# Seeding the scores' bank from VectorE instead of by a matmul, and a second bank for the values

## What is computed

```
# first: 128 latent tokens look at 2048 context tokens + the 128 latents, 16 heads of 64, batch 4
kv  = concat([xn @ Wkv, ln @ Wkv]);  k, v = split(kv)
qn, kn = rmsnorm(q) * scale, rmsnorm(k)
attn = softmax(qn @ kn.T  (masked));  out = attn @ v
# second: 128 tokens look at 2048 context tokens, 16 heads of 32, batch 4
score = (q @ k.T) / sqrt(32), masked with -1e9;  out = softmax(score) @ v
```

## Time and profile before

| | us |
|---|---|
| median of 3 runs | 2676.53 (2675.3 to 2676.94) |
| the profiled execution, its own time | 2673.37 |
| its span, first to last instruction | 2671.6 |
| mean granted TensorE clock | 0.948 of full speed |
| busy: PE, DVE, ACT, POOL | 2347.0, 1645.9, 1592.9, 1115.5 |

### The profile page before, as it was taken

How to read it: one execution, slowest core, us unless ns; L and a number is a source line. 1 busy time by engine, 2 the same in 40 slices (tenths; PEclk the granted TensorE clock), 3 DMA queues, 4 the chain that set the end, 5 groups by cost and what they waited for, 6 DMA issues and landing times. The chain is left out here.

```text
span 2671.6 us, 57444 instructions
## 1 busy us (share of the span) xinstructions
PE 2347.0 (88%) x21892; PEld 1526.2 (57%) x22210; DVE 1645.9 (62%) x3086; ACT 1592.9 (60%) x2934; POOL 1115.5 (42%) x896
## 2 busy tenths in 40 slices
PE   5389999999999999998688699995799899996885
PEld 2245666666666665655345477773567676774442
DVE  4466666666666655554146399995777777763126
ACT  3246666666666666666225288984477777777103
POOL 2345666556755675446100000003466666656000
PEclk9599999999999999999889799997999999997887
DMA  4322233223322231111352479994533434221302
GB/s 129 96 73 78 67 112 91 71 71 115 91 71 69 83 89 39 38 39 34 115 206 70 155 283 364 363 337 169 165 116 117 125 116 130 86 87 53 106 0 81
DMA packets 256291, 314.10 MB, mean 118 GB/s; under 512 B 71425, under 2 KB 182913, under 8 KB 255121
## 3 DMA queue, kind: packets, MB, share of 16 engines
q1 hardware_dynamic: 252064, 302.28, 35.4%
q10 hardware_dynamic: 3312, 6.03, 0.6%
q0 software_dynamic: 640, 2.10, 0.3%
HBM read 226.56 MB, written 48.10 MB: 103 GB/s over the span
## 5 line engine op out<-in xcount | busy, mean ns | idle before, releaser
L602 POOL TENSOR_TENSOR a_plo<-a_p,a_phi 128x512 bf16<-128x512 f32 x272 | 331.1, 1218 | 406.0 <-ACT a_phi L658 403.8
L788 PE MATMUL ps<-w_lo,a_xhi 128*128 128x512 bf16 x1078 | 409.7, 380 | 2.0 <-issue 0.2
L787 PE MATMUL ps<-w_hi,a_xhi 128*128 128x512 bf16 x1054 | 400.5, 380 | 2.6
L789 PE MATMUL ps<-w_hi,a_xlo 128*128 128x512 bf16 x1039 | 394.7, 380 | 0.5
L1937 POOL TENSOR_TENSOR a_plo<-a_p,a_phi 128x512 bf16<-128x512 f32 x256 | 303.1, 1184 | 179.9 <-ACT a_phi L1974 175.1
L624 ACT ACTIVATE a_kraw<-ps 128x256 f32<-128x256 f32 x272 | 104.2, 383 | 381.3 <-PE ps L789 378.7
L681 DVE TENSOR_TENSOR a_v<-ps,a_v 128x256 bf16<-128x256 f32 x272 | 114.7, 422 | 327.7 <-ACT a_v L626 327.5
L2069 DVE CUSTOM_DVE_ANT_0 a_junk<-ps,a_biasrow 128x512 bf16<-128x512 f32 x256 | 176.2, 688 | 115.6 <-PE ps L2184 88.1
L1969 ACT ACTIVATE a_p<-ps,a_mcol 128x512 f32<-128x512 f32 x256 | 174.9, 683 | 93.7 <-PE ps L2202 87.1
L561 POOL TENSOR_TENSOR a_rn<-a_rn,a_power 128x16 f32<-128x16 f32 (+1 forms) x80 | 204.0, 2550 | 6.6
L695 DVE SCALAR_TENSOR_TENSOR a_kraw<-a_kraw,a_rn 128x1024 f32<-128x1024 f32 (+1 forms) x80 | 129.7, 1621 | 92.7 <-POOL a_rn L561 92.7
(11 more groups left out here) (433 smaller groups left out, 6743.4 us busy)
## 6 DMA issues: line engine op xcount, KB each, us to landing
e_wst<-in_L_ffn_W SPq DMA_DIRECT2D x46, 2048.0 KB, 10.3
a_xn<-in_ctx SPq DMA_DIRECT2D x16, 1024.0 KB, 5.6
a_ks<-a_khi SPq DMA_DIRECT2D x256, 64.0 KB, 2.0
a_ks<-a_klo SPq DMA_DIRECT2D x256, 64.0 KB, 2.0
a_ct<-in_ctxT SPq DMA_DIRECT2D x16, 1024.0 KB, 5.9
a_ks<-k1h_d SPq DMA_DIRECT2D x128, 128.0 KB, 2.5
k1h_d<-a_khi SPq DMA_DIRECT2D x64, 128.0 KB, 2.0
k1l_d<-a_klo SPq DMA_DIRECT2D x64, 128.0 KB, 1.7
```

The costliest lines, as they stand in the source:

```text
L602: pool.tensor_tensor(p_lo[:, m % 3, :], p32[:, m % 2, :], p_hi[:, m % 3, :], ALU.subtract)\
L787: pe.matmul(out, x_hi[:, c, tile], w_hi[:, c, g, :], start=(c == 0), stop=False)
L788: pe.matmul(out, x_hi[:, c, tile], w_lo[:, c, g, :], start=False, stop=False)
L789: last = pe.matmul(out, x_lo[:, c, tile], w_hi[:, c, g, :], start=False, stop=(c == C - 1))
```

## The change

In the first cross attention the matmul of ones and `Dg` is issued once a unit (`less_maximum`, at the end of the step before the unit's first scores; twice for the first unit, to fill both banks) in place of once a tile. VectorE copies the filled bank to a bf16 tile `less` in SBUF (`seed` with s = 0) and for each of the unit's other 16 tiles copies `less` into the scores' bank (`seed` otherwise), one step ahead of the scores, right behind `values_low`. The scores' matmuls all have `start=False` and add to what is there. `scores` waits for `less_done` or `seeded` where it waited for `d_ready` and `exp_done`; the wait for `exp_done` is now VectorE's. `Dg` has one buffer in place of two.

In the second cross attention the values alternate between banks 2 and 7, and the row of maxima of unit u goes into the bank of its values ahead of them. `values` of a unit's first tile waits for `row_done` of its own unit, and `maximum_row` for `o_evac` of the unit two before.

```diff
-    Dg = sb("a0_d", [P, 2, 4, P], BF16)
+    Dg = sb("a0_d", [P, 4, P], BF16)
+    less = sb("a0_less", [P, 512], BF16)
...
-                    if u >= 2:
-                        dve.wait_ge(s_mm, NT0 * (u - 1))
+                    if u:
+                        dve.wait_ge(less_mm, u)
                     for i in range(4):
-                        dve.tensor_scalar(Dg[:, u % 2, i, :], identb[:], m4[:, i:i + 1], -1.0, ALU.mult, ALU.mult)\
+                        dve.tensor_scalar(Dg[:, i, :], identb[:], m4[:, i:i + 1], -1.0, ALU.mult, ALU.mult)\
                            .then_inc(d_ready, 1)
+
+            def seed(m):
+                u, s = divmod(m, NT0)
+                if s == 0:
+                    dve.wait_ge(less_mm, u + 1)
+                    if u:
+                        dve.wait_ge(seeded, (NT0 - 1) * u)
+                    dve.tensor_copy(less[:], ps[:, m % 2, :]).then_inc(less_done, 1)
+                    dve.wait_ge(less_done, u + 1)
+                else:
+                    if m >= 2:
+                        dve.wait_ge(exp_done, m - 1)
+                    dve.tensor_copy(ps[:, m % 2, :], less[:]).then_inc(seeded, 1)
...
                 if 0 <= n < N:
                     values_low(n)
+                if 0 <= n + 1 - LAG < N:
+                    seed(n + 1 - LAG)
...
             def scores(m):
                 u, s = divmod(m, NT0)
                 if s == 0:
-                    pe.wait_ge(d_ready, 4 * (u + 1))
+                    pe.wait_ge(less_done, u + 1)
+                else:
+                    pe.wait_ge(seeded, m - u)
+                out = ps[:, m % 2, :]
...
+            def less_maximum(u):
+                m = NT0 * u
+                pe.wait_ge(d_ready, 4 * (u + 1))
                 if m >= 2:
                     pe.wait_ge(exp_done, m - 1)
-                out = ps[:, m % 2, :]
-                tile = slice(s * P, (s + 1) * P)
-                pe.matmul(out, onesb[:], Dg[:, u % 2].rearrange("p h q -> p (h q)"), start=True, stop=False)
...
+                else:
+                    pe.matmul(ps[:, m % 2, :], onesb[:], Dg[:].rearrange("p h q -> p (h q)"), start=True, stop=False,
+                              skip_group_check=True).then_inc(less_mm, 1)
...
+                u, s = divmod(n + 1 - LAG, NT0)
+                if s == 0 and 0 <= u < UNITS:
+                    less_maximum(u)
...
+    def bank_v(u):
+
+        return (2, 7)[u % 2]
...
             def maximum_row(u):
                 pe.wait_ge(d_ready, 4 * (u + 1))
-                if u:
-                    pe.wait_ge(row_done, u)
-                pe.matmul(ps[:, ROW, :], onesb[:], Dg[:].rearrange("p h q -> p (h q)"), start=True, stop=True)\
+                if u >= 2:
+                    pe.wait_ge(o_evac, u - 1)
+                pe.matmul(ps[:, bank_v(u), :], onesb[:], Dg[:].rearrange("p h q -> p (h q)"), start=True, stop=True)\
                   .then_inc(row_mm, 1)
...
             def values(m):
                 u, s = divmod(m, NT)
                 if s == 0:
-                    if u:
-                        pe.wait_ge(o_evac, u)
+                    pe.wait_ge(row_done, u + 1)
...
-                    o = ps[:, PV, h * VW:(h + 1) * VW]
+                    o = ps[:, bank_v(u), h * VW:(h + 1) * VW]
```

More of the change, by code:

```diff
@@ L352, in cross0_attend @@
     mcol_ready, mrow_ready = sem("a0_mcol_r"), sem("a0_mrow_r")
+    less_mm, less_done, seeded = sem("a0_less_mm"), sem("a0_less_d"), sem("a0_seeded")
     max_mm, max_done, d_ready = sem("a0_max_mm"), sem("a0_max_done"), sem("a0_d_r")
@@ L829, in scores @@
                 if s == 0:
-                    pe.wait_ge(d_ready, 4 * (u + 1))
+                    pe.wait_ge(less_done, u + 1)
+                else:
+                    pe.wait_ge(seeded, m - u)
+                out = ps[:, m % 2, :]
+                tile = slice(s * P, (s + 1) * P)
+                for h in range(4):
+                    o = out[:, h * P:(h + 1) * P]
+                    pe.matmul(o, ks[:, u % 2, h, tile], q_both[:, u % 3, h, :], start=False, stop=False,
+                              skip_group_check=True)
+                    last = pe.matmul(o, ks[:, u % 2, h, tile], q_low[:, u % 3, h, :], start=False, stop=(h == 3),
+                                     skip_group_check=True)
+                last.then_inc(s_mm, 1)
+            def less_maximum(u):
+                m = NT0 * u
+                pe.wait_ge(d_ready, 4 * (u + 1))
                 if m >= 2:
                     pe.wait_ge(exp_done, m - 1)
-                out = ps[:, m % 2, :]
-                tile = slice(s * P, (s + 1) * P)
-                pe.matmul(out, onesb[:], Dg[:, u % 2].rearrange("p h q -> p (h q)"), start=True, stop=False)
[L836 to L840, removed]
+                if u == 0:
+                    pe.matmul(ps[:, 1, :], onesb[:], Dg[:].rearrange("p h q -> p (h q)"), start=True, stop=False,
+                              skip_group_check=True)
+                    pe.matmul(ps[:, 0, :], onesb[:], Dg[:].rearrange("p h q -> p (h q)"), start=True, stop=False,
+                              skip_group_check=True).then_inc(less_mm, 1)
+                else:
+                    pe.matmul(ps[:, m % 2, :], onesb[:], Dg[:].rearrange("p h q -> p (h q)"), start=True, stop=False,
+                              skip_group_check=True).then_inc(less_mm, 1)
             def values(m):
@@ L1794, in cross1_attend @@
     dve_step = sem("a1_dve")
-    PV, KP, VP, ROW = 2, 3, 4, 7
+    KP, VP = 3, 4
     N = NT * 4 * B
@@ L1960, in maximum_row @@
                 act.wait_ge(row_mm, u + 1)
-                act.activation(qs[3 * DH1:3 * DH1 + 1, u % 3, :], ps[3 * DH1:3 * DH1 + 1, ROW, :], ACT.Copy)\
+                act.activation(qs[3 * DH1:3 * DH1 + 1, u % 3, :], ps[3 * DH1:3 * DH1 + 1, bank_v(u), :], ACT.Copy)\
                    .then_inc(row_done, 1)
@@ L2082, in result @@
                 dve.wait_ge(pv_mm, NT * (u + 1))
-                o = ps[:, PV, 0:4 * VW].rearrange("p (h d) -> p h d", d=VW)
+                o = ps[:, bank_v(u), 0:4 * VW].rearrange("p (h d) -> p h d", d=VW)
                 step(dve.tensor_copy(o32[:], o[:, :, DH1 + 1:VW]))
```

## The result

The change takes the kernel from 2676.74 us (median of 4 runs, 2675.3 to 2681.61) to 2629.69 us (4 runs, 2626.5 to 2635.64): ratio 0.982, 95% interval 0.980 to 0.985, some 47 us or 1.8%. The same kernel run once more, in five rounds, gave 0.982 (0.9803 to 0.9837). The forecast was 2617.5 us with a range of 2605 to 2646: right direction, inside the range, 12 us too optimistic. The profiled execution of the changed kernel took 2635.64 us, the slowest of its four.

What follows compares the result with a forecast made beforehand. TensorE's list was taken to bound the first cross attention, and waits on VectorE's reciprocal to cost time in the second. 41.4 + 17.6 = 59.0 us took the median from 2676.5 to 2617.5 us, range 2605 to 2646.

Steps and rivals of the forecast that it cites:

- The bound: First cross attention, 217 to 1236 us: as long as TensorE's list; removing 231 matmuls of 0.216 us gives 49.9 us.
- The price of a copy: First cross attention: each VectorE copy into PSUM taken at 0.68 us, with 0.24 and 1.64 as the ends.
- (a): First cross attention, `Dg` matrices: 1.6 us lost once at the first unit; elsewhere 0.2 us slack, no cost.
- (b): First cross attention, scaled keys: scores wait for the copy; three mask units 1.0 us each, five groups 0.8 together: 3.8 us.
- (c): First cross attention, transposes' bank: copy ahead of the keys' low half costs 0.7 us at three places, 2.1 us.
- (d): End of first cross attention: last unit's lead copy has no projection to hide it, 1.0 us lost.
- Part 1 in sum: First cross attention, matmuls removed and copies added: 49.9 - 8.5 = 41.4 us gained.
- Part 2: Second cross attention, second bank for values: first values' wait for VectorE's reciprocal goes; 17.6 us stay, between nothing and 22.3.
- that just holds: Second cross attention: maxima three steps on need keys landing at 2151.7 us and would now come at 2151.8.
- the second bank's gain is given back: Rival, second cross attention: only the first unit's part and the last two stay; sum 41.4 us, kernel 2635 us; chance 0.11.
- The break-even: First cross attention: from 1.36 us a copy on, VectorE's unit exceeds the old 70.1 us plus 1.2 us given back.

Runs made afterwards that it cites:

- part 1 alone: The change's first cross attention with the old second one, against the kernel before: 2640.28 us, ratio 0.985, 41.0 us faster.
- later loads: Second cross attention's context and last two mask loads two steps later, first two masks one earlier; on the kernel before: ratio 0.9972, 6.9 us faster.
- part 2 alone: Only the second bank for values in the second cross attention, against the kernel before: 2667.51 us, ratio 0.995, 13.8 us faster.

## Why the prediction was right, and where it was off

**The bound.** Right. TensorE's list set the first stage: an ordinary unit went from 70.68 to 67.23 us, 3.45 us for 16 matmuls, 0.216 us each, with nothing held back. 231 x 0.216 = 49.9 us was really taken off.

**The price of a copy.** Taken at 0.68 us, measured at 682 ns (all 256 of the changed kernel: minimum/median/maximum in ns, first and last start in us):

```profile
L751 DVE CAST ps<-a_less x256: 675/682/695, 220.2 to 1239.7; 128x512 f32<-128x512 bf16 x128
```

The row nearest in size and kind, L1521, was the right one. The spread is 20 ns while GpSimd is busy 612 of 978 us, so there is no contention, and GpSimd's low half L606 kept its 1.16 us. The rule of the Trainium skill (SBUF — State Buffer, "Who interferes with whom") that one SBUF input outside the two-port modes is not disturbed by GpSimd agrees with this trace. The up to twice faster copy that the Trainium skill's table (VectorE: DVE Perf Modes, "The perf-mode tier table") allows for an operand in PSUM did not show: a bf16 copy into an f32 bank took as long as the f32 copy out of one (684 ns). The same section of the Trainium skill takes that rate back for fp32 operands in PSUM, to the single rate, and the copy's output is fp32; so page and trace agree, and the prediction's estimate of some 0.4 us had overlooked that half of the rule.

**(a) the diagonal matrices.** Forecast 1.6 us once, and 0.2 us of slack elsewhere; measured 1.6 us once (the unit in whose course the scores begin took 63.47 us after 63.43 before, though seven matmuls of 0.216 us fewer are in it: nine L835 are gone, two of the new ones have come) and no loss in ordinary units. Right.

**(b) and (c) the scaled keys and the transposes' bank.** The places were right, the sizes not. The five milder places of (b) cost nothing: with VectorE waiting for the root anyway, the copies fit in. The three units with masks were to lose 1.0 + 0.7 us each and lost 2.7 us each, 8.2 in all; all but 1.3 us of it goes when the mask stands one step later. For (c), TensorE came 1.31 us late, where 0.7 had been worked out. The step that failed is that I read each slack by itself: mask, root, scaling, copy and low half stand in one chain, and TensorE, now faster, is late there even without the copies (4.0 of the 8.2 us). Forecast 5.9 us, measured 8.2.

**(d) the end.** From the last projection to the last scores 41.7 us in the profile before and 46.0 after, which looks like 4.3 us. But three other profiles in which this stage is unchanged have 44.3, 43.8 and 44.3 us. The four of before's stage have a mean of 43.5, the five with part 1 and the old masks 44.5, 46.0, 45.1, 43.9 and 44.9, mean 44.9: a loss of 1.4 us, no more than the profiles of either kind differ among themselves. Forecast 1.0. A single pair of profiles would have misled here.

**Part 1 in sum.** 49.9 - 1.6 - 8.2 - 1.4 = 38.7 us; the stage's means are 1162.8 and 1124.4 us, 38.4 us apart. Forecast 41.4. That the median of part 1 alone gave 41.0 us is in part luck.

**Part 2.** The wait on the reciprocal went, and an unhindered unit is 1.30 to 1.35 us shorter (33.67 to 32.37 us from one row of maxima to the next), as forecast. But 17.6 us became 10.4 in the stage alone (601.2 to 590.8) and 13.8 by the medians. The step that failed is "that just holds": I had set the keys' reads 0.1 us from late by one place, landing 2.5 us after their issue, gave what I found there to ten units, and did not look where SyncE's list has masks and a megabyte ahead of the writes. At those three places the reads are themselves issued 6.3 to 8.3 us after the second write in the changed kernel, in place of 1.7. The largest interval between two rows of maxima in the change, with the wait of 3.95 us, is 39.25 us (before, 34.35), though only 34.25 in the second profile of the same kernel. This is the rival "the second bank's gain is given back", in part: 4 to 7 us of 17.6. The loads' place explains only 1 to 2 us of these (with later loads part 2 alone gives 11.9 us in the stage in place of 10.4, and 15.9 in place of 13.8 by the medians); they cost the kernel before as well. A term for the loads the prediction did not have at all.

**What stays open.** With later loads part 2 gives 11.9 us (597.2 to 585.3) or, on top of part 1, 14.4 (597.0 to 582.6), not 17.6. In three of 14 intervals between rows of maxima (the first, fifth and ninth) it gains next to nothing there (32.68 us with it and 32.69 without; 33.62 against 33.67; 33.85 against 33.69), and which loop holds these I did not find. Whether part 1 lengthens the second stage by moving it against the loads, or the single profiles only fell so, is open, and so is what gave back the masks' gain in part 1 alone. "Later loads" moves the context and the masks together; which of the two matters more no run shows.

**The break-even.** 1.36 us a copy was worked out from a unit's total of work, with part 2's gain counted in; for part 1 alone it is 1.29. At 1.32 us ordinary units came out at 70.5 to 71.1 us, close to that sum. But the kernel lost 17 us, in the mask units and the tail, where others wait for single results of VectorE. An engine in such a place costs time before it is full: here at 88% of the stretch on the mean, 91% of an ordinary unit, while 82% cost an ordinary unit nothing.

## What to carry to other kernels

An engine with slack can take work off the bounding one, and the sum "instructions removed times their issue interval" is good to a per cent as long as each added instruction has a place where its engine waited anyway. What is lost stands at few places, where several short slacks lie in one chain; look for the rare instructions (here a mask once a batch) that stand ahead of such a chain, and move those first. And when a stage gets faster, follow the DMAs that share a queue with its own round trips: moving the loads by one or two steps was worth 10 us on top of the change here, and 7 us without it.

## What the runs showed of the hardware that was not expected

A write of 128 KB issued within 3 us behind a 1 MB load on the same engine's list took far longer than such a write mostly does. In the changed kernel such writes of keys landed 3.6 to 8.2 us after their issue; the others took 1.7 us in the median, and none more than 4.5. The reads that wait for both writes were issued 8.3 us after the second write in one place, and 6.4 us in one of the kernel before. The page of the changed kernel shows the sizes (KB each, median us to landing), and the view of L1895, the second write, how far one can be from its median:

```profile
a_ct<-in_ctxT SPq DMA_DIRECT2D x16, 1024.0 KB, 6.6
a_ks<-k1h_d SPq DMA_DIRECT2D x128, 128.0 KB, 2.5
k1h_d<-a_khi SPq DMA_DIRECT2D x64, 128.0 KB, 2.0
k1l_d<-a_klo SPq DMA_DIRECT2D x64, 128.0 KB, 1.7
...
DMA to landing us min/median/max: 1.7/1.7/8.2
```

And values that VectorE writes into a bank of PSUM are added to by matmuls that do not start the bank anew, once an earlier matmul has started it; each unit of the change rests on that in 16 of its 17 tiles.
